# Logits product over the column groups, stacked weights written in pieces, and gates scaled after the decode instead of before

## The reference

```python
z = jnp.einsum('nd,sdr->nsr', xf, P)
scores = jnp.einsum('nsr,smr->nsm', z, C)
topv, topi = jax.lax.top_k(scores, K)          # K = 4
w = jax.nn.softmax(topv, axis=-1)
h = jax.nn.gelu(jnp.einsum('nsr,nskrh->nskh', z, W1g) + b1g)
yl = jnp.einsum('nskh,nskhr->nskr', h, W2g) + b2g
comb = jnp.einsum('nskr,nsk->nsr', yl, w)
out = jax.nn.gelu(comb @ G1 + g1b) @ G2 + g2b
```

## Time and profile before

| what | value |
| --- | --- |
| median of 3 runs | 1491.64 us (1490.36 to 1491.73) |
| the profiled execution's own time | 1490.83 us |
| its span, first to last instruction | 1488.9 us |
| busy: PE, DVE, ACT, POOL | 1279.1 (86%), 1162.5 (78%), 1083.9 (73%), 1057.5 (71%) |
| chain that ended last, by engine | ACT 32%, PE 28%, DVE 24%, issue 7%, POOL 3%, DMA 3% |
| mean granted clock of PE | 0.944 of full speed |

### The profile page before, as it was taken

The page is one execution under the profiler, slowest core; times in us unless marked ns, Lnnn a source line. Parts: engine busy times, 40 slices in busy tenths (PEclk is TensorE's granted clock), DMA queues, the critical chain, the costliest instruction groups (busy, mean ns, idle before and its releaser), DMA issues.

```text
span 1488.9 us, 34181 instructions
## 1 busy us (share of the span) xinstructions
PE 1279.1 (86%) x12216; PEld 650.2 (44%) x12216; DVE 1162.5 (78%) x3407; ACT 1083.9 (73%) x2675; POOL 1057.5 (71%) x771
## 2 busy tenths in 40 slices
PE   4743888889888888886699999999999999999996
PEld 3632555555555665553233333333333333333332
DVE  5671388888888888886688888888888888888884
ACT  1242355556655556553599999999999999999995
POOL 6660367667666666664488888888888888888885
PEclk8865899999999999997599999999999999999998
DMA  9635412221121111223312313223132131322310
GB/s 267 134 97 75 63 33 65 66 81 60 57 66 62 58 57 59 63 72 86 94 40 46 79 45 86 60 47 83 45 82 60 46 84 45 81 60 46 86 40 12
DMA packets 93640, 103.81 MB, mean 70 GB/s; under 512 B 12244, under 2 KB 90604, under 8 KB 93190
## 3 DMA queue, kind: packets, MB, share of 16 engines
q1 hardware_dynamic: 89120, 92.76, 24.3%
q10 hardware_dynamic: 2240, 5.08, 2.4%
q0 software_dynamic: 2112, 3.79, 1.1%
HBM read 64.83 MB, written 33.52 MB: 66 GB/s over the span
## 4 chain that ended last, share of the span: by engine, by line
ACT 32%; PE 28%; DVE 24%; issue 7%; POOL 3%; DMA 3%; SPq 2%; ACTq 1%; POOLq 0%; DVEq 0%
ACT ring L1016 19%; ACT arena L1028 9%; PE ring L1642 7%; PE code L1655 6%; DVE arena L1207 5%; DVE arena L1408 4%; PE ring L1528 4%; DVE arena L1196 3%; PE ring L1498 2%; DVE arena L1216 2%; PE ring L1539 2%; PE ring L1674 2%; DMA arena<-in_x 1%; ACT arena L884 1%; DVE arena L1288 1%
## 5 line engine op out<-in xcount | busy, mean ns | idle before, releaser
L1408 DVE TENSOR_TENSOR arena<-ring,arena 128x496 f32<-128x496 f32 x1008 | 611.5, 667 | 132.6 <-ACT ring L1016 131.4
L800 POOL TENSOR_TENSOR arena<-arena 128x992 f32<-128x992 f32 x264 | 608.5, 2315 | 122.7 <-ACT arena L1028 113.3
L1016 ACT ACTIVATE ring<-ring 128x496 f32<-128x496 f32 x1008 | 549.1, 701 | 10.3 <-PE ring L1642 10.3
L1642 PE MATMUL ring<-arena,w_stack 99*32 99x496 bf16 x6144 | 427.8, 376 | 26.6 <-DVE arena L1408 20.9
L1655 PE MATMUL code<-arena,w_pad 128*32 128x496 f32 x3072 | 389.6, 581 | 3.7 <-ACT arena L1032 3.4
L1642 PEld LDWEIGHTS ring<-arena,w_stack 99*32 99x32 bf16 x6144 | 160.4, 95 | 410.5 <-DVE arena L1408 239.4
L1028 ACT ACTIVATE arena<-ring 128x992 f32<-128x992 f32 x252 | 287.0, 1139 | 0.0
L1498 PE MATMUL ring<-arena 96*128 96x372 f32 x384 | 142.0, 502 | 9.1 <-ACT arena L898 7.7
L1655 PEld LDWEIGHTS code<-arena,w_pad 128*32 128x32 f32 x3072 | 96.5, 110 | 56.5 <-DVE arena L1408 17.9
L733 POOL TENSOR_TENSOR arena<-arena 128x372 f32<-128x372 f32 x96 | 91.7, 975 | 37.1 <-DVE arena L1257 36.8
L1498 PEld LDWEIGHTS ring<-arena 96*128 96x128 f32 x384 | 72.7, 197 | 79.1 <-issue 25.7
(11 more groups left out here) (134 smaller groups left out, 1666.8 us busy)
## 6 DMA issues: line engine op xcount, KB each, us to landing
arena<-gates SPq DMA_DIRECT2D x48, 496.0 KB, 6.7
gates<-arena SPq DMA_DIRECT2D x16, 744.0 KB, 10.5
arena<-h_scratch SPq DMA_DIRECT2D x32, 279.0 KB
arena<-z_parts SPq DMA_DIRECT2D x144, 62.0 KB, 2.3
h_scratch<-arena SPq DMA_DIRECT2D x16, 279.0 KB
z_parts<-arena SPq DMA_DIRECT2D x48, 93.0 KB, 1.8
arena<-h_scratch SPq DMA_DIRECT2D x12, 372.0 KB
out_h<-arena SPq DMA_DIRECT2D x12, 372.0 KB
```

What stands on the lines that cost most here:

```text
L800: p_.tensor_tensor(gated[:, quad % SPACES, j:j + 2], hid[:, POOL_DUOS.index(duo) % 2], gst[:, block // EB, j:j + 2], ALU.mult).then_inc(s_ ...
L1016: a_.activation(product, product, ACT.Gelu_apprx_tanh).then_inc(s_hid, 1)
L1408: v_.tensor_tensor(gated[:, quad % SPACES, j + p], duo_bank(duo, p), gst[:, block // EB, j + p], ALU.mult).then_inc(s_gat, 1)
L1642: mm = t_.matmul(bank[32 * q:32 * q + 32], w1s[:, x + 32 * q:x + 32 * q + 32], zst[:, o, j + p], start=True, stop=True)
```

## The change

Four things are changed.

1. **Logits product.** The loops of `logits` change places: the chunk c is the outer loop, the sequence b (the column group) the inner one.
2. **Stacked weights.** `stack_w1` goes. Its nine DMAs are issued by ACT in pieces: parts 0, 3 and 5 in the embedding stage behind `mean_off` of text steps 8, 9 and 10; parts 1 and 4 in pass 0 behind w copies 3 and 4; part 2 in pass 1 behind w copy 3; the bias rows in pass 1 behind w copies 4 and 5.
3. **Gates.** POOL's `gates` and DVE's three `raw_sum` and three `raw_recip` a pass go; the raw gates are transposed and stored. The sum of the four best exponentials is made apart: DVE subtracts the maximum from the four best (`top4_shifted`, 124 x 96), ACT applies exp (`top4_exp`), DVE sums (`top4_summed`) and inverts (`scales_made`); PE transposes the 24 columns (`scales_transposed`), ACT copies (`copy_scales`), SP stores (`store_scales`) to a new array of 8 x 5952 scales.
4. **Scale after the decode.** In the code stage SP loads the scales of a tile, each row repeated over 16 partitions, beside the biases; POOL adds the biases and then multiplies with the scales in a second instruction.

The diff, cut to its core:

```diff
+STACK_PARTS = {(0, 3): 1, (0, 4): 4, (1, 3): 2}
+STACK_BIASES = {(1, 4): (0,), (1, 5): (1, 2)}
...
 def stage2_over(eng):
...
+            wait(eng, s_rd, 16 * UNITS)
...
+            def store_scales(u):
+                wait_apart(sp, (s_rt, u + 1))
+                sp.dma_start(rq_u[u], rt).then_inc(s_rd, 16)
...
             def pass_sp(i):
...
                 if has(i - 3):
                     store_bias(i - 3)
+                    store_scales(i - 3)
                 if has(i - 1):
                     store_h1(i - 1)
...
             def load_bias(tile):
                 wait_apart(sp, (s_cb, tile))
                 sp.dma_start(bias_t, bq[:, bass.ds(tile * TN, TN)]).then_inc(s_bl, 16)
+                sp.dma_start(scale_t, rq[:, bass.ds(tile * TN, TN)].unsqueeze(1).to_broadcast([S, R, TN])).then_inc(s_bl, 16)
...
             def pass_pool(i):
...
                 if has(g):
                     z_part3(g)
-                    gates(g, 0)
                     shift(g, 2)
                 if has(b):
                     residual_biased(b)
-                if has(g):
-                    gates(g, 1)
-                    gates(g, 2)
                 if has(a + 1):
                     rstd("A", a + 1, EPS_LN)
...
             def add_bias(tile):
-                wait_apart(pool, (s_comb, tile + 1), (s_bl, 16 * (tile + 1)))
-                p_.tensor_tensor(code, comb, bias_t, ALU.add).then_inc(s_cb, 1)
+                wait_apart(pool, (s_comb, tile + 1), (s_bl, 32 * (tile + 1)))
+                p_.tensor_tensor(biased, comb, bias_t, ALU.add).then_inc(s_ba, 1)
+                pool.wait_ge(s_ba, tile + 1)
+                p_.tensor_tensor(code, biased, scale_t, ALU.mult).then_inc(s_cb, 1)
...
             for jj in range(JJ):
                 mean_off(jj)
+                if jj >= 8:
+                    act.wait_ge(s_wc, 1)
+                    stack_part((0, 3, 5)[jj - 8])
...
             def copy_bias(u):
                 act.wait_ge(s_bp, u + 1)
+                act.wait_ge(s_rp, u + 1)
...
+            def top4_exp(u):
+                act.wait_ge(s_vd, u + 1)
+                wait(act, s_gs, u)
+                a_.activation(vx, vd, ACT.Exp).then_inc(s_vx, 1)
...
             def pass_act(i):
...
-                if not has(a - 1) and has(a):
-                    stack_w1()
...
+                    if (i, c) in STACK_PARTS:
+                        stack_part(STACK_PARTS[i, c])
+                    if (i, c) in STACK_BIASES:
+                        for p in STACK_BIASES[i, c]:
+                            stack_bias(p)
                 if has(g - 1):
                     copy_bias(g - 1)
+                    copy_scales(g - 1)
                 if has(g):
                     scores_exp(g, 2)
+                    top4_exp(g)
                     gates_copy(g, 0)
...
+            def top4_shifted(u):
+                dve.wait_ge(s_v8, SUB * (u + 1))
+                wait(dve, s_vx, u)
+                v_.tensor_tensor(vd, v8[:, :, :, 0:4], v8[:, :, :, 0:1].to_broadcast([ST, SUB, S, 4]),
+                                 ALU.subtract).then_inc(s_vd, 1)
...
                     raw(g, 0)
                     mark(g, 1)
-                    raw_sum(g, 0)
                     top8(g, 2)
-                    raw_recip(g, 0)
                     top4(g, 2)
                     raw(g, 1)
+                    top4_shifted(g)
                     mark(g, 2)
                 if has(a):
                     norms_floored(a)
-                if has(g):
-                    raw_sum(g, 1)
-                if has(a):
                     norms_inverted(a)
-                if has(g):
-                    raw_recip(g, 1)
-                if has(a):
                     head_weights(a)
                 if has(g):
                     raw(g, 2)
+                    top4_summed(g)
                 if has(a + 1):
                     dve.wait_ge(s_x0, 16 * (a + 2))
                     bn_stats("A", a + 1, x0)
                 if has(g):
-                    raw_sum(g, 2)
+                    scales_made(g)
                 if has(a + 1):
                     bn_aggr("A", a + 1)
-                if has(g):
-                    raw_recip(g, 2)
...
+            def scales_transposed(u):
+                pe.wait_ge(s_gr, u + 1)
+                t_.transpose(pair1[0:SUB * S, 0, UT:UT + ST], gr.rearrange("p a b -> p (a b)"),
+                             ident[0:ST, 0:ST]).then_inc(s_rp, 1)
...
             def logits(u):
                 pe.wait_ge(s_L, u + 1)
                 wait(pe, s_bt, u - 2)
-                for b in range(UB):
-                    for c in range(CH):
+                wait(pe, s_rt, u - 2)
+                for c in range(CH):
+                    for b in range(UB):
                         last = t_.matmul(pair1[32 * b:32 * b + 32, 0, 0:N], lsel[:, b, c],
-                                         wsq[:, c, N * b:N * b + N], start=(c == 0), stop=(c == CH - 1))
+                                         wsq[:, c, N * b:N * b + N], start=(c == 0), stop=(c == CH - 1),
+                                         skip_group_check=True)
...
             def gates_transposed(u, s):
                 pe.wait_ge(s_z1, u + 1)
-                pe.wait_ge(s_gg, SUB * u + s + 1)
+                pe.wait_ge(s_gu, SUB * u + s + 1)
...
                 if has(g - 1):
                     bias(g - 1)
+                    scales_transposed(g - 1)
```

More of the change, by code:

```diff
@@ L321, in build @@
         bias_t = c3(128, [TN])
+        scale_t = c3(128, [TN])
+        biased = c3(128, [TN])
         h1t = c3(ST, [TSUB, D])
@@ L903, in copy_bias, with copy_scales @@
                 act.wait_ge(s_bp, u + 1)
+                act.wait_ge(s_rp, u + 1)
                 wait(act, s_bd, 16 * u)
                 a_.copy(bt, pair1[:, 0, 0:UT]).then_inc(s_bt, 1)
+            def copy_scales(u):
+                act.wait_ge(s_rp, u + 1)
+                wait(act, s_rd, 16 * u)
+                a_.copy(rt, pair1[0:SUB * S, 0, UT:UT + ST]).then_inc(s_rt, 1)
             def z_copies(u):
@@ L1004, in _ @@
             copy_bias(UNITS - 1)
+            copy_scales(UNITS - 1)
             stage2_over(act)
@@ L1218, in raw, with top4_summed, scales_made @@
                                         op0=ALU.is_equal, op1=ALU.mult).then_inc(s_gu, 1)
[L1220 to L1226 removed]
+            def top4_shifted(u):
[3 more added lines that the diff above has]
+                                 ALU.subtract).then_inc(s_vd, 1)
+            def top4_summed(u):
+                dve.wait_ge(s_vx, u + 1)
+                v_.tensor_reduce(gs, vx, AX.X, ALU.add).then_inc(s_gs, 1)
+            def scales_made(u):
+                dve.wait_ge(s_gs, u + 1)
+                wait(dve, s_rp, u)
+                v_.reciprocal(gr, gs).then_inc(s_gr, 1)
             def pi_recip(u):
```

43 lines of the change are left out of this document (19 added, 24 removed).

## The result

The changed kernel takes 1478.58 us (median of 3, 1476.38 to 1478.76) where the kernel before took 1491.64: a ratio of 0.991, 95% interval 0.989 to 0.993. It is faster, as forecast, but by 13.1 us instead of 29.7, and outside the range of 1446 to 1473. The profiled execution took 1476.38 us (span 1474.3), mean granted clock 0.939, before 0.944.

The account below looks back on a forecast made before the run. A chain of waits through several engines was taken to bound the attention stage, ACT the code stage. Terms -22.0 - 7.7 + 1.0 - 0.8 - 3.1 + 1.3 + 1.6 = -29.7 against 1491.64 gave 1462 us, range 1446 to 1473.

Parts of the forecast that it names:

- The product and the chain ahead of it: Steady attention passes: 0.25 us gained up to the head weights, 1.32 at the logits product; fourteen passes, -22.0 us.
- the lock on raw(1) and top4_shifted: Steady pass: POOL's shift stops DVE's raw(1) (about 1.5 us), POOL's residual stops top4_shifted (about 1.2).
- Rival B: Logits product: column groups do not run side by side in an accumulating chain; about 1486 us; chance 0.08.
- Rival A: Steady passes: the lock does not bite raw(1) and top4_shifted, PE becomes the limit; 1448 us; chance 0.14.
- the 22.6 us forecast for the stretch: Forecast terms between the logits products of passes 1 and 15, fourteen steady passes: -22.6 us.
- rival D: Steady passes: PE, with less work, falls to 1.2 GHz, some 11 us a pass; 1528 us with six; chance 0.04.
- The prediction's own sign of being wrong: Wrong if the logits product stays near 3 us, the pass above 33, or top4_shifted takes 0.2.
- Code stage: POOL's second instruction costs 1.3 us behind the last tile and 0.15 in each of eleven others, +1.6 (bounds 0 and 5).
- Passes 0 and 1: Earlier w copies (-3.0) and shorter logits products, less 0.9 for pieces in pass 1: -7.7 us, bounds -11 and -3.
- Stage 1: Embedding stage: part 5's 512 KB moved close to the last text stores, 0 to +3 us, taken +1.0.
- End of the stage: Last attention passes: pass 16 no longer waits for POOL, -0.8; pass 17 loses lock, sum, reciprocal and POOL, -3.1.
- Rival C: Steady passes: half the product's gain is given back at the loop's next wait, 14 x 0.66; 1471 us; chance 0.13.

Follow-up runs that it names:

- the fill: Changed kernel plus eight small matmuls that compute nothing, in TensorE's idle time behind spread_pi(2) and spread_pi(3) of each gate-unit pass: 1459.45 us, ratio 0.977.

## Why the prediction was right and wrong

**The product and the chain ahead of it: right.** The product 1.17 us (1.2 forecast), DVE the later one, 1.84 behind the head weights (1.93), the lock on raw(1) and top4_shifted (1.54 and 1.26), a short pass of 31.88 (32.04). Rival B (column groups not side by side) is excluded by the 48 records in 1.17 us. The rule of the Trainium skill ("TensorE: Matmul & The Clock Gate", Part 3, The mechanism) that weight loads overlap running matmuls only where the row group differs does not fit this trace: all of these share their rows, and four loads and four matmuls start within 22 ns, at 371.90. The measurement decides. Rival A (no lock) is excluded by the 1.26. Of the 22.6 us forecast for the stretch, 21.4 are there once the clock is held.

**The step that failed** is the one that gave rival D 0.04: "the busy share would only fall from 0.88 to 0.86". The share did what it said (130.55 of 150 us, 0.87), and the clock fell all the same. The step judged the clock by an average over 150 us and took the twelve passes between 250 and 650 us for alike, though two of them lasted 35.29 us and one 34.29, each with a stretch at 0.50. The price was wrong too, on the other side: 11 us a pass assumed the whole pass at 1.2 GHz, where one fall lasts 3.4 us and costs 1.66. The trace of before had what a better bound needs: passes longer by 1.7 us with a fall behind PE idle times of 1.35 and 0.73 us. One fall in each of the 14 passes, ten more than before, would be 17 us. (The order alone came to that.) It did not have the number itself: why ten falls and not four is open. All that the runs say is that the shorter product adds 0.47 us of idle time near them. The prediction's own sign of being wrong, a pass above 33 us, came true in nine passes of 14. Measured: the 461.3 us are 15.0 above 14 x 31.88, the nine long passes at 1.66; the 473.6 of before are 3.0 above 14 x 33.62; the clean passes gave 14 x (33.62 - 31.88) = 24.4; 24.4 - 15.0 + 3.0 = 12.4, which is the 12.3 of the table.

**Code stage: the place right, the term mis-sized.** Forecast 0.15 us a tile with an upper bound of 0.46; measured 0.52, so 5.7 for 1.6 in eleven tiles, and 1.4 behind the last gelu (1.3 forecast). Up to the first copy_code the profile has 0.9 more, which is scatter: 68.8 to 70.3 us in the changed kernel's relatives, 69.1 to 69.6 in those of the kernel before. Laid beside the run without the multiplication, instruction by instruction, ACT's whole delay in a tile is made at two gelus: 0.14 to 0.19 at duo 18, which the forecast left out (duo 12's buffer is late by then), and 0.43 more at duo 20, close to the 0.46 that it worked out. It counted on ACT's overlap and its later waits for PE to cover two thirds of that. They cover little: the delay is 0.6 us behind duo 20 and 0.5 to the end of the tile, through two waits for PE of 0.3 and 0.6 us that are as long as without it.

**Passes 0 and 1.** -5.8 forecast up to the product of pass 1, -10.5 measured. The pieces' share is the one mis-sized: -3.0 forecast up to the product of pass 0, -6.4 measured (27.3 to 20.9 us from the first bn_stats, with the pieces alone too). From there to the product of pass 1 -2.8 was forecast (-3.7 and +0.9) and -4.1 measured. (Two small steps of the forecast are off by 0.1: 5.82 less 2.2 is 3.6, and 512 KB at 95 GB/s take 5.5 us.) **Stage 1:** +1.0 for +3.5, of which 0.9 lies behind the last gather in this profile (up to 3 in others) and the rest is scatter of the gathers. **End of the stage:** -5.2 forecast behind the product of pass 15, -3.3 measured. The order alone has -4.5 there and all but the order -3.8, so the shares don't add up; no run settles why.

**Rival C** (half of the product's gain given back, 9 us, 1471) was near the missing 10.3 in size, for a wrong reason: no wait of the loop took it, as the fill shows.

## What to carry to other kernels

Before shortening TensorE's work in a loop, look at the granted clock pass by pass, not in a mean over many: if single passes already show a fall behind short idle times, the change can bring more (here ten for four) or hardly any more (five, in passes shorter still), and the price is the slowed pieces behind the idle time. The code stage says the same: an edit that made TensorE wait 2.26 us in a tile brought falls where there had been none. A few matmuls that compute nothing, placed where TensorE waits, are then a cheap trial. Parts of a change should be timed together as well as alone: here neither half alone shortened the steady passes, and both together did.

## What the runs showed of the hardware

- The clock fell to 0.50 for 3.4 us behind idle stretches of PE of no more than 1.40 us (the first fall of the changed kernel, of the fill and of the order alone apart, behind 2.23, 2.23 and 4.30 us), in some passes and not in others with the same idle times to the hundredth. Which pass is hit the runs don't settle: 4, 10, 6, 14 and 5 falls in kernels whose clean passes last 33.6, 31.9, 33.3, 32.5 (estimated) and 30.9 us, so their number doesn't follow the length of the pass. By the new idle time ahead of the first spread_pi there were 4, 4 and 6 falls in the kernels without it, 5 to 10 in the four with 0.47 us and no fill, and 14 in the one with 0.81: more on the whole, but each number is from one profile, and no run changes that idle time alone.
- A VectorE instruction with one input in PSUM took 0.67 us beside GpSimd, and one of the same size with both in SBUF 2.75; 96 elements a partition took 1.26 us beside GpSimd's residual, and 0.25 behind it. The Trainium skill ("SBUF — State Buffer", Who interferes with whom) says that a VectorE instruction with two inputs in SBUF contends with a GpSimd instruction that reads SBUF, and one with at most one such input, outside the 2-port modes, does not; these runs agree.
- Four column groups of TensorE that accumulate over six chunks run side by side: 1.17 us for 3.16, 2.7 times faster.
